# A two-layer relational graph convolution: the stores of y asked for by ScalarE, the last product's roots and scaling one tile back

## The reference, cut to what matters

```python
def _rgcn_conv(x, src, dst, etype, W, root, b):      # x: 1250 x 768, 21250 edges, 8 relations
    x_src = x[src]
    seg = dst * num_rel + etype
    sums = jax.ops.segment_sum(x_src, seg, num_segments=num_nodes * num_rel)
    cnt = jax.ops.segment_sum(ones, seg, num_segments=num_nodes * num_rel)
    mean = sums / jnp.maximum(cnt, 1.0)[:, None]
    mean = mean.reshape(num_nodes, num_rel, -1)
    out = jnp.einsum('nri,rio->no', mean, W)
    return out + x @ root + b

h = _rgcn_conv(x, src, dst, edge_type, W1, root1, b1)
h = jax.nn.relu(h)
out = _rgcn_conv(h, src, dst, edge_type, W2, root2, b2)
x = _layernorm(x + out, axis=-1)
```

## Time and profile before

| | |
|---|---|
| Median of three runs | 1454.06 us |
| The profiled execution, its own time | 1466.17 us |
| Its span, first to last instruction | 1464.3 us |
| Mean granted clock of TensorE | 0.994 |
| Busy share PE, DVE, ACT, POOL | 98%, 63%, 39%, 38% |
| y stores asked for by SP | 640 DMAs |
| Weight loads asked for by SP | 37 DMAs |

### The profile page before, as it was taken

The page is one execution under the profiler, slowest core; times in us unless marked ns, Lnnn a source line. Parts: engine busy times, 40 slices in busy tenths (PEclk is TensorE's granted clock), DMA queues, the critical chain, the costliest instruction groups (busy, mean ns, idle before and its releaser), DMA issues.

```text
span 1464.3 us, 23621 instructions
## 1 busy us (share of the span) xinstructions
PE 1437.1 (98%) x8715; PEld 1419.6 (97%) x8715; DVE 927.6 (63%) x1475; ACT 573.1 (39%) x805; POOL 559.0 (38%) x437
## 2 busy tenths in 40 slices
PE   8999999999999899999999999999999999999997
PEld 8999999999999899999999999999999999999996
DVE  7899999857777577456771154545454454444677
ACT  4222334335444444344552233333343333433454
POOL 0000000066777686425535232434242424243552
PEclk9999999999999999999999999999999999999998
DMA  6414321358877776664463465646464656656454
GB/s 195 152 60 127 96 72 47 106 183 267 254 211 227 227 229 191 212 200 149 136 189 103 148 211 168 210 144 218 142 211 156 199 177 184 194 171 213 119 169 123
DMA packets 112523, 248.58 MB, mean 170 GB/s; under 512 B 19617, under 2 KB 87768, under 8 KB 112446
## 3 DMA queue, kind: packets, MB, share of 16 engines
q0 software_dynamic: 30880, 134.67, 31.1%
q1 hardware_dynamic: 81566, 112.88, 24.1%
HBM read 192.77 MB, written 65.49 MB: 176 GB/s over the span
## 4 chain that ended last, share of the span: by engine, by line
PE 89%; DVE 6%; issue 3%; ACT 1%; DMA 1%; SPq 0%; ACTq 0%; POOLq 0%
PE prod L767 70%; PE agg L809 14%; DVE g_low L1029 2%; PE agg L904 2%; PE agg L767 2%; PE prod L809 1%; PE agg L758 1%; DVE g_high L1029 1%; ACT g_high L628 1%; DVE acc L1046 1%; DVE g_low L1033 1%; DMA x_rows<-in_x 0%; PE agg L907 0%; DVE stats L1401 0%; DMA raw<-y,bucket_index 0%
## 5 line engine op out<-in xcount | busy, mean ns | idle before, releaser
L767 PE MATMUL prod<-w_high,h_high 128*128 128x384 f32 x2064 | 693.5, 336 | 0.0
L767 PE MATMUL prod<-w_high,h_low 128*128 128x384 f32 x2064 | 690.4, 335 | 0.0
L767 PE MATMUL prod<-w_low,h_high 128*128 128x384 f32 x2064 | 690.1, 334 | 0.0
L519 POOL DMA_INDIRECT raw<-y,bucket_index x310 | 410.5, 1324 | 538.5 <-DVE g_low L1033 220.1
L653 ACT ACTIVATE y_stage<-prod 128x384 f32<-128x384 f32 x320 | 157.7, 493 | 781.6 <-PE prod L767 631.1
L1033 DVE TENSOR_TENSOR g_low<-raw,g_high 128x768 fp32r<-128x768 f32 x240 | 220.4, 956 | 370.6 <-ACT g_high L631 312.4
L767 PEld LDWEIGHTS prod<-w_high,h_high 128*128 128x128 f32 x2064 | 388.1, 188 | 0.1
L767 PEld LDWEIGHTS prod<-w_low,h_high 128*128 128x128 f32 x2064 | 388.0, 188 | 0.0
L767 PEld LDWEIGHTS prod<-w_high,h_low 128*128 128x128 f32 x2064 | 387.8, 188 | 0.0
L631 ACT ACTIVATE g_high<-raw 128x768 fp32r<-128x768 f32 x240 | 189.9, 839 | 1.9 <-DMA raw<-y,bucket_index 1.5
L809 PE MATMUL agg<-g_high,one_hot 128*128 128x384 f32 x616 | 159.8, 340 | 10.1 <-DVE g_low L1033 7.6
(11 more groups left out here) (179 smaller groups left out, 992.7 us busy)
## 6 DMA issues: line engine op xcount, KB each, us to landing
y<-y_stage SPq DMA_DIRECT2D x320, 168.0 KB
w_raw<-in_w_all SPq DMA_DIRECT2D x35, 1152.0 KB
y<-y_stage SPq DMA_DIRECT2D x320, 19.5 KB
raw<-y,bucket_index POOLq DMA_INDIRECT x310
acc<-in_x POOLq DMA_DIRECT2D x10, 375.0 KB, 6.4
x_rows<-in_x SPq DMA_DIRECT2D x10, 336.0 KB
out<-acc SPq DMA_DIRECT2D x10, 336.0 KB
w_raw<-in_w_all SPq DMA_DIRECT2D x2, 576.0 KB, 4.6
```

The lines of the kernel that those rows point to most:

```text
L519: pool.indirect_dma_start(raw_rows(slot), None, y[0:written * N, :], bass.IndirectOffsetOnAxis(ap=bucket_index[:, at_column:at_column + 1] ...
L767: mm = pe.matmul(to, left[:, k, t * P:(t + 1) * P], right[:, h, k, :], start=(k == 0 and left is h_high and right is w_high), stop=(n == 0 ...
```

## The change

`store_y` moves from the program of SP to that of ACT. ACT's `matrix` calls it right behind `stage_y`: ACT waits for its own staging (y_staged), and asks for the two DMAs of the step on its own queue. SP keeps the weight loads, the tables and the output; `load_unit` now waits for nothing but w_high and w_low of the half before. In `finish` of layer 2, `deviation` and `norm` of a tile (ACT) and `scale_of` (DVE) stand one tile further back: ACT's first g_high of tile t+1 is followed by the root of tile t-1, the other g_high, and the scaling of tile t-1.

```diff
@@ -401,26 +401,13 @@
                 w = w_all[bass.ds(m, 1), :, h * HALF:(h + 1) * HALF].rearrange("o (k p) n -> p (o k) n", p=P)
                 sp.dma_start(w_raw[:], w).then_inc(w_loaded, 16)
 
-            def store_y(yc, r, s):
-
-                h, t = divmod(s, T)
-                sp.wait_ge(y_staged, STEPS * yc + s + 1)
-                for rows in parts_of(t):
-                    sp.dma_start(y[bass.ds(r * N + t * NT + rows.start, rows.stop - rows.start),
-                                   h * HALF:(h + 1) * HALF],
-                                 y_stage[rows, s % BANKS, :]).then_inc(y_stored[s % BANKS], 16)
-
-            def relation(q, yc, r):
-                for s in range(STEPS):
-                    store_y(yc, r, s)
-                    if isinstance(q, int) and q == TABLE_END and s == 3:
-                        sp.wait_ge(flags_counted, 1)
-                        sp.dma_start(inv_table.rearrange("(p k) o -> p (k o)", p=P), inv_count[:])\
-                            .then_inc(inv_stored, 16)
-                    if s == 8:
-                        load_unit(q + 1, 0)
-                    if s == 14:
-                        load_unit(q + 1, 1)
+            def relation(q):
+                if isinstance(q, int) and q == TABLE_END:
+                    sp.wait_ge(flags_counted, 1)
+                    sp.dma_start(inv_table.rearrange("(p k) o -> p (k o)", p=P), inv_count[:])\
+                        .then_inc(inv_stored, 16)
+                load_unit(q + 1, 0)
+                load_unit(q + 1, 1)
 
             def load_x(t):
                 if t >= 2:
@@ -446,7 +433,6 @@
             for s in range(STEPS):
                 if s + 4 < T:
                     load_x(s + 4)
-                store_y(0, 0, s)
                 if s == 8:
                     load_unit(1, 0)
                 if s == 10:
@@ -459,17 +445,17 @@
                 if s == 14:
                     load_unit(1, 1)
             for q in range(1, ROOT1):
-                relation(q, q, q)
+                relation(q)
                 if q == TABLE_END:
                     sp.wait_ge(bucket_added, 2 + T)
                     sp.dma_start(bias[:], b2.rearrange("(o n) -> o n", o=1).to_broadcast([P, D]))\
                         .then_inc(bias_loaded, 16)
             load_unit(ROOT1 + 1, 0)
             load_unit(ROOT1 + 1, 1)
-            relation(ROOT1 + 1, stored_before(1, 0), 0)
+            relation(ROOT1 + 1)
             with sp.Fori(1, R - 1) as r:
-                relation(r + ROOT1 + 1, stored_before(1, r), r)
-            relation(ROOT2 - 1, stored_before(1, R - 1), R - 1)
+                relation(r + ROOT1 + 1)
+            relation(ROOT2 - 1)
             for t in range(T):
                 sp.wait_ge(*((normed, t + 1) if t < T - 1 else (last_normed, 1)))
                 for rows in parts_of(t):
@@ -653,7 +639,16 @@
                 act.activation(y_stage[:, s % BANKS, :], prod[:, bank, 0:HALF], ACT.Copy)\
                     .then_inc(y_staged, 1)
 
-            def matrix(q, yc, actions=lambda s: [], after=None):
+            def store_y(yc, r, s):
+
+                h, t = divmod(s, T)
+                act.wait_ge(y_staged, STEPS * yc + s + 1)
+                for rows in parts_of(t):
+                    act.dma_start(y[bass.ds(r * N + t * NT + rows.start, rows.stop - rows.start),
+                                    h * HALF:(h + 1) * HALF],
+                                  y_stage[rows, s % BANKS, :]).then_inc(y_stored[s % BANKS], 16)
+
+            def matrix(q, yc, r, actions=lambda s: [], after=None):
 
 
                 for s in range(STEPS):
@@ -661,6 +656,7 @@
                         if what == "sum":
                             bucket(g, t)
                     stage_y(yc, STEPS * q + s, s, bank_of(s))
+                    store_y(yc, r, s)
                     for what, turn, _, t in actions(s):
                         if what == "turn":
                             high_of_turn(turn, t)
@@ -687,8 +683,8 @@
             act.wait_ge(w_loaded, 16)
             act.activation(w_high[:, 0, K // 2:K], w_raw[:, K // 2:K], ACT.Copy).then_inc(w_high_ready, 1)
             high_of_turn(0, 1)
-            matrix(0, 0, turning_x)
-            matrix(1, 1)
+            matrix(0, 0, 0, turning_x)
+            matrix(1, 1, 1)
 
             def copy_keys(c):
                 act.wait_ge(rows_counted, 1)
@@ -718,16 +714,21 @@
                 for t in range(T):
                     if layer == 0 and t == T - 2:
                         high_of_unit(q + 1, 0, STEPS * q + FIRST_HALF)
-                    if t + 1 < T:
-                        bucket(g, t + 1)
+                    rows = list(enumerate(tile_range(g, t + 1))) if t + 1 < T else []
+                    for b, i in rows[:1]:
+                        high_of_tile(g, i, tiles(g) * (t + 1) + b)
+                    if layer and t:
+                        deviation(t - 1)
+                    for b, i in rows[1:]:
+                        high_of_tile(g, i, tiles(g) * (t + 1) + b)
                     if layer == 0:
                         relu(t)
-                        if t:
-                            high_of_turn(1, t - 1)
-                    else:
-                        deviation(t)
-                        if t + 1 < T:
-                            norm(t)
+                    if layer == 0 and t:
+                        high_of_turn(1, t - 1)
+                    if layer and t:
+                        norm(t - 1)
+                if layer:
+                    deviation(T - 1)
 
             def deviation(t):
                 act.wait_ge(var_ready, t + 1)
@@ -738,15 +739,15 @@
                 act.activation(acc[:, t, :], acc[:, t, :], ACT.Identity, bias=shift[:, t % 2, :],
                                scale=std[:, t % 2, 1:2]).then_inc(normed, 1)
 
-            matrix(2, 2, after=copied_ahead(2))
-            matrix(3, 3, after=copied_ahead(3))
+            matrix(2, 2, 2, after=copied_ahead(2))
+            matrix(3, 3, 3, after=copied_ahead(3))
             for q in range(TABLE_END, ROOT1 - 1):
-                matrix(q, q, pair_of(q))
-            matrix(ROOT1 - 1, ROOT1 - 1, one_relation(R - 2, None))
+                matrix(q, q, q, pair_of(q))
+            matrix(ROOT1 - 1, ROOT1 - 1, R - 1, one_relation(R - 2, None))
             finish(0)
-            matrix(ROOT1 + 1, stored_before(1, 0), last_turns)
+            matrix(ROOT1 + 1, stored_before(1, 0), 0, last_turns)
             with act.Fori(1, R) as r:
-                matrix(r + ROOT1 + 1, stored_before(1, r), one_relation(r + R - 1, None))
+                matrix(r + ROOT1 + 1, stored_before(1, r), r, one_relation(r + R - 1, None))
             finish(1)
 
 
@@ -1365,18 +1366,19 @@
                     if t + 1 < T:
                         cut_low(g, t + 1, 0, 1)
                     if (layer, t) == (1, T - 1):
+                        scale_of(t - 1)
                         last_moments(g, t)
                         continue
                     add(g, R - 1, t)
+                    if layer and t:
+                        scale_of(t - 1)
                     if t + 1 < T:
                         cut_low(g, t + 1, 1)
                     if layer:
                         moments_of(t)
                     if t + 2 < T:
                         mark(g, R - 1, t + 2)
-                    if layer and t + 1 < T:
-                        scale_of(t)
-                    elif layer == 0 and t:
+                    if layer == 0 and t:
                         low_of_turn(1, t - 1)
 
             def scale_of(t):
```

## The result

The changed kernel takes 1516.08 us (median, 1515.35 to 1519.22) where the kernel before takes 1454.03 beside it: ratio 1.043, interval 1.041 to 1.045. That is 62.0 us slower. The forecast was 1497, range 1467 to 1522: the sign and the mechanism of the loss held, the size was 19 us short (1516.1 against 1497).

A forecast was written before the change was run, and what follows sets the result against it. PE, busy 98%, was taken to bound the kernel, with ACT's g_high allowed only a small delay before PE waits. Losses 57.3 - 6.6 - 0.9 - 6.5 = +43.3 us on 1454.06 gave 1497 us, range 1467 to 1522.

The forecast's parts named there:

- narrow buckets: Eight buckets of ten, staging one bare product (3.1 us) ahead; margin before PE waits 0.48 us, a relation's first 0.30.
- The first rival: ACT's requests cost next to nothing, delay 0.45 us in the loop and 0.25 outside: 1443 us; chance 0.12.
- The fourth: Rival: the clock falls in the new gaps, once in a relation, 22 us more: 1519 us; chance 0.06.
- One sign: In layer 2's loop PE would wait for DVE's g_low some 0.75 us at each narrow bucket, 56 of them.
- Layer 2's loop, 44.4 + 3.3 us: Loss over seven relations: 44.4 us at the buckets, 3.3 us from the late w_high of step 1.
- 8 x 1.25 - 7 x 0.48 - 0.30: Loop loss per relation: eight g_high delays of 1.25 us less margins of seven buckets and the first, 6.3 us.
- The w_high of step 1: In the loop it follows that step's stores, making step 2's staging 0.47 us late: 7 x 0.47 = 3.3 us.
- q = 7, 3.6 us: Unrolled, seven narrow buckets each losing a delay of 1.0 us less 0.48 of margin: 3.6 us.
- q = 4 to 6, 6.0 us: Delay of 1.0 us covered by a margin of 1.86, except behind w_high, twice in each: 6.0 us.
- The credits for SP's queue, -6.6 and -0.9 us: Gains from stores no longer behind SP's wait for w_low: -6.6 us in q = 5, -0.9 us in q = 7.
- third rival: The stores gain nothing from leaving SP, as requests share the same DMA engines: 1505 us; chance 0.10.
- Part 2, -6.5 us: Finish of layer 2, roots and scaling one tile back: tiles -3.0 us, last bucket and what follows -3.5 us.

The follow-up runs named there:

- the third experiment: Changed kernel with ACT asking for the store of step s - 1 just ahead of staging s, behind the g_high in between: 1445.43 us.
- the ninth experiment: Changed kernel with three requests per store (112, 6 and 7 rows) in place of two: 1550.83 us.
- part 2 alone: Kernel before with only the last product's roots and scaling one tile back, stores still on SP: 1446.13 us.
- the second profile of before: Kernel before, unchanged, run once more for a second profiled execution: 1454.38 us.
- the eighth experiment: Changed kernel with the stores of layer 2 given back to SP, those of layer 1 still on ACT: 1460.87 us.

## Why the prediction was right, and where its sizes were off

**Right: what bounds, and the sign.** The chain from staging over g_high and g_low to the bucket was the thing to read, and the third experiment shows that it is all of the loss. The price of a request, taken from SP's rows, was right (0.317 against 0.323 us), and so was the delay in the loop: 1.25 us against 1.18 to 1.20 at most narrow buckets, and up to 1.5 at a few. The first rival (requests next to free) is false at 0.32 us each. The fourth is false for this kernel: the clock stayed at 1.00 through the loop with gaps of 1.05 to 1.20 us at the first bucket of every relation. The mechanism is real: in the ninth experiment it comes with gaps of 1.9 us. One sign came out otherwise than named: PE's rows show 0.4 to 0.5 us of idle time at most narrow buckets, not 0.75, the rest being booked as longer matmuls.

**Layer 2's loop, 44.4 + 3.3 us: 56.5 measured.** The step that failed is "8 x 1.25 - 7 x 0.48 - 0.30". Delay and margin in it are right. Over one relation the delays by the rows of the eight buckets come to 9.7 to 10.3 us (the step has 10.0) and the margins, in part 2 alone, to 3.65 (3.66), so the difference is 6.0 to 6.6. Missing is what it costs PE to start again. A bucket whose two halves each wait lasts 0.80 us from the start of its second half to the next product, not 0.69, and laid beside part 2 alone, each narrow bucket loses about 0.13 us more than delay less margin. Eight of these are 1.0 us a relation, 7 us in all. The w_high of step 1 costs its 0.47 us and a little more: the first bucket alone loses 1.6 us. In effect the margin was near 0.35, not 0.48 us: an estimate, 0.48 less 0.13. The row that could have told it stood in the earlier trace rows: a bucket that has waited shows 0.62 us for two matmuls, one that has not 0.51.

**q = 7, 3.6 us: 6.1 measured**, with the root behind it. The term has seven narrow buckets; there are eight, and each loses 0.66 us (1.01 - 0.48 + 0.13). That gives 5.3. By the stagings the first of them loses 1.0, behind the w_high of step 1, one 0.78, and the last with the root behind it 0.96, which makes the 6.1.

**q = 4 to 6, 6.0 us: 6.5 measured.** Of the six places behind w_high, PE waits 0.93 us at five; the sixth is q = 4's first bucket, where its gap grew from 1.29 to 2.31 us. Laid beside part 2 alone each of the six costs 1.0 us, as the step has it, the restart included. One more wait in the middle of q = 4, 0.59 us, costs another 1.0, and 0.9 us come back at the start of q = 6, as said below.

**The credits for SP's queue, -6.6 and -0.9 us: at most 0.9.** This is the other step that failed, and it is a misreading, not a size. The stall was real in the one execution that was profiled, and the prediction saw that this execution lay 12.1 us over the median; it then took the difference as an offset that before and after share, and booked the removal of a stall against runs which did not have it. The stall does go: in the changed kernel ACT never waits for a stored buffer. But in the second profile of before that wait is 4.68 us, and PE does not feel it; in that of part 2 alone it is 5.3 us, and PE waits 0.65 us, a stretch that the changed kernel passes 0.9 us sooner. The third experiment, with nothing of the stores on SP, is 0.7 us faster than part 2 alone, which is within the noise. So the prediction's third rival, the stores gaining nothing, was right on this term. Between the two profiled executions the difference is only 1515.35 - 1466.17 = 49.2 us, because the first of them has the stall; that this lies nearer the forecast's 43.3 is no support for it.

**Part 2, -6.5 us: -6.7 alone, -7.1 in the profiles.** The tiles give 2.7 us (3.0 predicted), the last tile and the tail behind it 4.4 (3.5), which the clock helped.

The sum, from profiles: 12.9 for all ahead of the loop, 56.5 for the loop, -7.1 for the last product, 62.3 where the medians have 62.0. Against the forecast: 8.8 in the loop, 7.5 of credits that were not there, 3.3 in the losses ahead of the loop (12.9 for 9.6, the 0.9 us already taken off), less 0.6 for part 2: 19.0, where the medians say 62.0 - 43.3 = 18.7. That the time fell inside the range owes something to its width: the two failed steps, 8.8 and 7.5 us, pointed the same way.

## What to carry to other kernels

An engine at 39% may still be the wrong place for a request: ask what stands behind it in that engine's queue and how much slack that has, here 0.5 us. If it must be there, put it behind the instruction that others wait for; here the same 640 requests then cost nothing. And when the profiled execution lies a per cent over the median, look for a stall that only it has before booking its removal.

## What was not expected of the hardware

- **A wait can hide in busy time.** With one request per store the bucket's first matmuls show 0.1 us of idle time and 379 ns in place of 335, while each relation loses 3.1 us. A matmul that starts behind a wait is shown longer (0.61 us for two, 0.51 undisturbed). The rows above also leave room for it: undisturbed matmuls start 0.17 us apart and are shown 0.33 us long, so PE can start one 0.16 us late without any idle time in its rows.
- **A second request costs more than the first.** Single requests of 125 rows took 0.27 us of ACT's queue, two of 112 and 13 rows 0.80: 0.32 each and 0.16 between. A third, of a store cut into 112, 6 and 7 rows, added 0.40.
- **The queue of an engine runs ahead of its arithmetic.** In the third experiment ACT's two requests ran at 926.84 and 927.33, while its g_high of 926.57 to 928.15 computed; a request whose wait is already satisfied hid behind arithmetic entirely.
- **The length of a gap alone does not decide whether the clock falls.** With three requests per store the granted clock fell to its lower level, 1.2 GHz, behind first-bucket gaps of 1.86, 1.94 and 1.97 us and stayed at 2.4 GHz behind others of 1.88 and 1.98; in q = 4 it stayed there behind 2.31 us in the changed kernel (1.00 from 315 to 322 us) and fell behind the same gap in the eighth experiment (0.76 from 316 to 323 us). What else decides is not shown.
